# NF4 chunks dequantised in turned layout, and two chunks' accumulator in PSUM

## The chip, the core and the metric

The kernel runs on 1 core of a Trainium2 chip. The metric is device time in microseconds of one execution. Engines are named TensorE (PE), VectorE (DVE), ScalarE (ACT), GpSimd (POOL) and SyncE (SP, which issues most DMAs).

## What is computed

```python
x = x + xattn(layernorm(x), ctx, ctx, mask, Wq, Wk, Wv, Wo)   # 32 query heads, 8 key heads of 128, tanh cap 30
x = x + ffn(layernorm(x), w1, w2, w3)
# ffn: each weight is first quantised and dequantised in blocks of 64 along its rows
absmax = max(abs(flat), axis=1)              # flat = w.reshape(-1, 64)
idx = searchsorted(bounds, flat / absmax)    # 15 bounds, 16 NF4 codes
dq = NF4_CODE[idx] * absmax
out = (silu(x @ dq1.T) * (x @ dq2.T)) @ dq3.T
```

x is 8 x 128 x 512, w1 and w2 are 1376 x 512, w3 is 512 x 1376, all fp32. Blocks of 64 run along the 512 columns of w1 and w2 and along the 1376 columns of w3.

## The kernel before, in words

**Attention.** All 1024 tokens lie in SBUF as `xh` and `xl` (a high and a low fp32r part), features on partitions; a product of two fp32 matrices is three fp32r matmuls (high x high, high x low, low x high). After 16 key units and 16 value units the loop runs over 64 slots j = 8 kv + b (8 key heads, 8 batches). TensorE does in a slot: four transposes of the attention result into `trp`, `weighted_values(j+1)` (L610), `logits(j+3)` (L583), `q_unit(j+8)` (L506, 12 matmuls of 512 columns), `out_unit(j)` (L519, 12 matmuls; it waits for `at_lo`, written by VectorE's `atl`). VectorE does (L1151): `add_out(j-1)`, one NF4 add, `atl`, `sums`, more adds, the mask of j+3, `rope_parts(j+8)`, one more add. The query swap goes through a DMA of SP (L341) and the rope is added by GpSimd (L1290) two slots or more before its logits. Slots 56 to 63 have no `q_unit` and no NF4 work.

**NF4.** The weights are cut into 12 chunks of 128 x 1408 (22 blocks of 64). For a chunk c VectorE takes the blocks' maxima, replaces zeros and inverts (`nf_prepare`, L962); GpSimd multiplies the chunk by the inverse, a 128x22 tile read as a broadcast (`nf_normalise`, L1319, by `nf_blocks`, L1314); ScalarE makes 15 sign masks in u8, five buffers ahead (`nf_above_bound`, L755, the activation is L766); VectorE adds 15 steps to the accumulator (`nf_add`, L975; the first add is L984, the other 14 are L987: `scalar_tensor_tensor` with mask and accumulator in SBUF); GpSimd multiplies by the maxima (`nf_rescale`, L1324); SP stores the result to DRAM (`nf_store`, L327). `nf_before(slot)` (L259) spreads the places of the list, 16 to a chunk (15 adds and a gap), over slots 1 to 56 of the loop, the 22 hidden units and the first W3 pieces. Chunk 0 is the first of W3, 1 to 8 are W1 and W2, 9 to 11 the rest of W3.

**FFN.** 22 pieces of W1/W2 (`weights_in`, L435) and 11 of W3 (`w3_in`, L452) come back from DRAM into `stage`, rows of the weight on partitions. TensorE turns each with four transposes (`weight_transposes` L647, `w3_transposes` L705, both through `transpose4` L501, whose matmul is L503); ScalarE copies the high part out of PSUM (L881, L903), VectorE makes the low part (L1202, L1234). `hidden(n)` is 24 matmuls for gate and up of 512 tokens; the down projection is 11 rounds of 7 batches x 3 matmuls, and then batch 7 alone. W3 piece 8 needs the last chunk: its 13 last adds follow `hidden(21)` on VectorE.

PSUM has 8 banks: `prjs` 2, `bank` 3, `avp` 2, `trp` 1.

## Time and profile before

| | |
|---|---|
| median of 3 runs | 800.41 us (800.33 to 800.9) |
| profiled execution | 800.16 us, span 798.3 us |
| granted TensorE clock | 1.00 |
| ScalarE, GpSimd busy | 547.4 us, 367.3 us |
| DMA | 87.56 MB, mean 110 GB/s |
| stages by the trace | keys and values to about 150 us, loop with queries to 558, last head to 596, hidden units to 730, down projection to the end |

A share of busy time is of the whole span; TensorE's matmuls overlap, so its busy time says that it seldom stood still, not that it ran at its peak.

### The profile page before, as it was taken

The numbers are of one execution on the slowest core, as the hardware profiler recorded it, in microseconds if no ns is written. First come the engines' busy times: TensorE is split into PE (matmuls) and PEld (weight loads), VectorE is DVE, ScalarE is ACT, GpSimd is POOL, SyncE is SP. The second block draws the span as 40 slices with busy tenths as digits, with TensorE's granted clock in tenths as the row PEclk, the third lists the DMA queues.
The fourth block names the chain that finished last, engine by engine and source line by source line (L and its number), as shares of the span: only waits on it lengthen the run. The fifth ranks groups of instructions, "written<-read, shape, count | busy, mean of one in ns | idle before, by whom it ended". The sixth has DMA issues, their size and how long they took to land.

```text
span 798.3 us, 10879 instructions
## 1 busy us (share of the span) xinstructions
PE 789.0 (99%) x3810; PEld 635.9 (80%) x3810; DVE 661.7 (83%) x741; ACT 547.4 (69%) x859; POOL 367.3 (46%) x210
## 2 busy tenths in 40 slices
PE   8999999999999999999999999999999999999998
PEld 6777887878887788878888888888778888888876
DVE  6897755898999999898988889899574999999913
ACT  6467737787877868678787788786643877868510
POOL 4773265446637457366465365473100534435010
PEclk9999999999999999999999999999999999999999
DMA  9636456333432433425235335231401031412022
GB/s 335 199 129 201 131 155 169 110 99 93 139 107 77 154 97 112 129 71 171 79 84 152 92 93 165 80 103 47 136 14 40 27 126 54 124 28 76 14 69 106
DMA packets 60981, 87.56 MB, mean 110 GB/s; under 512 B 6272, under 2 KB 29952, under 8 KB 60928
## 3 DMA queue, kind: packets, MB, share of 16 engines
q1 hardware_dynamic: 59744, 84.06, 35.7%
q10 hardware_dynamic: 1184, 2.82, 1.0%
q8 instruction: 31, 0.51, 0.3%
q14 instruction: 22, 0.18, 0.1%
HBM read 51.00 MB, written 19.07 MB: 88 GB/s over the span
## 4 chain that ended last, share of the span: by engine, by line
PE 85%; DVE 6%; issue 5%; ACT 2%; DMA 1%; POOL 0%; POOLq 0%; SPq 0%; DVEq 0%
PE bank L530 7%; PE prjs L514 7%; PE prjs L516 7%; PE bank L532 7%; PE bank L531 7%; PE prjs L515 7%; PE bank L590 7%; PE avp L618 6%; PE trp L503 4%; PE bank L496 3%; PE bank L498 3%; PE bank L497 3%; PE prjs L498 2%; PE prjs L496 2%; PE prjs L497 2%
## 5 line engine op out<-in xcount | busy, mean ns | idle before, releaser
L1294 POOL TENSOR_TENSOR qT<-cs_loop,sw 128x512 f32<-128x512 f32 x56 | 107.2, 1915 | 183.4 <-DMA sw<-cs_loop 176.1
L514 PE MATMUL prjs<-xh,wqh 128*128 128x512 f32 x256 | 123.3, 482 | 0.0
L530 PE MATMUL bank<-woh,ath 128*128 128x512 f32 x256 | 100.8, 394 | 1.0 <-DVE atl L1161 0.9
L516 PE MATMUL prjs<-xh,wql 128*128 128x512 f32 x256 | 100.2, 391 | 0.0
L532 PE MATMUL bank<-woh,atl 128*128 128x512 f32 x256 | 99.9, 390 | 0.0
L531 PE MATMUL bank<-wol,ath 128*128 128x512 f32 x256 | 99.7, 389 | 0.0
L862 ACT ACTIVATE ath<-trp 128x512 fp32r<-128x512 f32 x64 | 38.2, 596 | 89.5 <-PE trp L503 89.5
L515 PE MATMUL prjs<-xl,wqh 128*128 128x512 f32 x256 | 99.5, 389 | 0.0
L995 DVE TENSOR_TENSOR cs_loop<-prjs,csq 128x1024 f32<-128x1024 f32 x56 | 68.3, 1220 | 21.4 <-PE prjs L516 21.2
L987 DVE SCALAR_TENSOR_TENSOR nfv<-nfq,nfv 128x1408 f32<-128x1408 uint8 x42 | 79.1, 1883 | 0.2
L850 ACT ACTIVATE nrm<-avp,rs 128x128 f32<-128x128 f32 x256 | 72.6, 372 | 7.0 <-DVE rs L1148 6.7
L987 DVE SCALAR_TENSOR_TENSOR nfx<-nfq,nfx 128x1408 f32<-128x1408 uint8 x42 | 75.9, 1807 | 0.0
L1388 POOL TENSOR_TENSOR hl<-hf,hh 128x512 fp32r<-128x512 f32 x22 | 33.8, 1538 | 75.7 <-ACT hh L901 75.7
L766 ACT ACTIVATE nfq<-nfv,bnd 128x1408 uint8<-128x1408 f32 x45 | 66.1, 1477 | 3.0 <-POOL nfv L1316 3.0
L618 PE MATMUL avp<-vcur,eb 128*128 128x129 f32 x512 | 67.7, 275 | 0.0
L1120 DVE TENSOR_TENSOR eb<-bank,maskf 128x512 f32<-128x512 f32 x64 | 43.1, 673 | 28.1 <-ACT bank L844 28.1
L590 PE MATMUL bank<-qT,kcur 128*128 128x512 f32 x128 | 65.6, 594 | 0.6 <-DVE eb L1120 0.6
L766 ACT ACTIVATE nfq<-nfa,bnd 128x1408 uint8<-128x1408 f32 x45 | 65.6, 1475 | 0.4 <-POOL nfa L1316 0.4
L515 PEld LDWEIGHTS prjs<-xl,wqh 128*128 128x128 f32 x256 | 48.2, 188 | 21.9 <-issue 13.6
L514 PEld LDWEIGHTS prjs<-xh,wqh 128*128 128x128 f32 x256 | 48.2, 188 | 21.4 <-issue 13.6
L618 PEld LDWEIGHTS avp<-vcur,eb 128*128 128x128 f32 x512 | 62.3, 192 | 0.5 <-issue 0.5
L1285 POOL TENSOR_TENSOR wol<-stage,woh 128x512 fp32r<-128x512 f32 x32 | 58.5, 1830 | 8.8 <-ACT woh L784 8.8
(187 smaller groups left out, 1966.6 us busy)
## 6 DMA issues: line engine op xcount, KB each, us to landing
sw<-cs_loop SPq DMA_DIRECT2D x112, 128.0 KB, 2.3
stage<-wq_pieces SPq DMA_DIRECT2D x32, 256.0 KB, 2.9
stage<-wo_pieces SPq DMA_DIRECT2D x32, 256.0 KB, 3.1
stage<-dq_scratch SPq DMA_DIRECT2D x32, 256.0 KB, 3.2
ks_scratch<-qT SPq DMA_DIRECT2D x16, 256.0 KB, 3.1
vs_scratch<-vst SPq DMA_DIRECT2D x16, 256.0 KB, 3.5
kcur<-ks_scratch SPq DMA_DIRECT2D x16, 256.0 KB, 2.9
vcur<-vs_scratch SPq DMA_DIRECT2D x16, 256.0 KB, 3.4
```

What stands on the lines that cost most here:

```text
L514: nc.tensor.matmul(o, wqh[:, g, k, :], xh[:, k, cs], start=k == 0, stop=False)
L515: nc.tensor.matmul(o, wqh[:, g, k, :], xl[:, k, cs], start=False, stop=False)
L516: last = nc.tensor.matmul(o, wql[:, g, k, :], xh[:, k, cs], start=False, stop=k == KT - 1)
L530: nc.tensor.matmul(o, ah, wh[:, g, :], start=g == 0, stop=False)
L531: nc.tensor.matmul(o, ah, wl[:, g, :], start=False, stop=False)
L532: last = nc.tensor.matmul(o, al, wh[:, g, :], start=False, stop=g == G - 1)
L590: nc.tensor.matmul(lgp[:, :], kcur[:, h, s * 128:(s + 1) * 128], qT[:, h, :, s * 128:(s + 1) * 128], start=True, stop=True).then_inc(logit ...
L618: av = nc.tensor.matmul(avp[:, g // 2, (g % 2) * (DH + 1):(g % 2 + 1) * (DH + 1)], eb[:, b % 2, g * 128:(g + 1) * 128], vcur[:, b, :], sta ...
L766: nc.scalar.activation(nf_mask(c, i), nf_bufs(c)[0][:, :], ACT.Sign, bias=bnd[:, i:i + 1])\
L850: last = nc.scalar.activation(nrm[:, j % 2, g * 128:(g + 1) * 128], avp[:, g // 2, (g % 2) * (DH + 1):(g % 2) * (DH + 1) + DH], ACT.Copy, ...
L987: op = nc.vector.scalar_tensor_tensor(acc[:, :], nf_mask(c, i), STEPS[i], acc[:, :], ALU.mult, ALU.add)
L1294: nc.gpsimd.tensor_tensor(dst, products(ru, slot)[:, 0, :], sw[:, slot, :], ALU.add).then_inc(roped, 1)
```

## The change

W1, W2 and W3 are given to the kernel a second time: `nf_chunks` now holds the chunks turned (what the matmuls want on partitions lies on partitions), `nf_natural` holds the old layout. VectorE takes maxima and inverses from the natural chunk (`nf_top`, 12 of them, all but two in the loop). For each chunk of W1/W2 TensorE turns the 128x44 tile of maxima and inverses (`turn_tops`), ScalarE copies it to `rows` (`tops_rows`), SP stores it to DRAM (`rows_store`), and broadcast loads bring it back as a full 128x1408 tile `scl` (`scale_load`), once with the inverses and once with the maxima. For W3 this is done for all four chunks at once, with 32 stores. GpSimd multiplies by `scl`. Adds, masks and stores of a chunk work on the turned layout; the pieces that come back need no transposes, and ScalarE and VectorE read them from `stage`. The order is now W1/W2 in chunks 0 to 7 and W3 in 8 to 11; the loop takes chunks 1 to 8 whole. PSUM `bank[2]`, `avp` and `trp` become one tensor `four`; 1408 columns of it are the accumulator of chunks 9 and 10 for the adds 0 to 13, and TensorE waits for the end of chunk 10 before its down matmuls of batch 4. `nomask` and `keep` share the memory of `eb`. The core of the diff:

```diff
-        bank = [ctx.enter_context(nc.psum_tensor(f"bank{i}", [128, 512], f32)) for i in range(3)]
-        avp = ctx.enter_context(nc.psum_tensor("avp", [128, 2, 512], f32))
-        trp = ctx.enter_context(nc.psum_tensor("trp", [128, 512], f32))
-        prj, prj2, lgp = [prjs[:, 0, :], prjs[:, 1, :]], [bank[0], bank[1]], bank[2]
+        bank = [ctx.enter_context(nc.psum_tensor(f"bank{i}", [128, 512], f32)) for i in range(2)]
+        four = ctx.enter_context(nc.psum_tensor("four", [128, 4, 512], f32))
+        lgp, avp, trp = four[:, 0, :], four[:, 1:3, :], four[:, 3, :]
+        prj, prj2 = [prjs[:, 0, :], prjs[:, 1, :]], [bank[0], bank[1]]
+        wide = four.rearrange("p b n -> p (b n)")[:, 0:CH]
         key_pair = [prjs, avp]
...
+        ADDS = [(c, i) for c in range(1, 12) for i in range(15)]
+        STREAM = [x for n, add in enumerate(ADDS)
+                  for x in ([(n // 9 + 2, None)] if n % 9 == 0 and n < 90 else []) + [add]]
+        LOOP_ITEMS = STREAM.index((9, 0))
...
-                return 122 * min(max(0, slot - 1), 55) // 55
+                return LOOP_ITEMS * min(max(0, slot - 1), 55) // 55
             if slot <= NSTEP + 2 * HT:
-                return 122 + 43 * min(max(slot - NSTEP - 2, 0), 20) // 20
-            return min(165 + max(0, 3 * (slot - NSTEP - 2 * HT) - 1), 16 * 11)
+                return LOOP_ITEMS + 34 * min(max(slot - NSTEP - 2, 0), 20) // 20
+            return min(LOOP_ITEMS + 34 + max(0, 3 * (slot - NSTEP - 2 * HT) - 1), len(STREAM))
...
+        def nf_norms(slot):
+
+            return [c + 1 for c, i in nf_items(slot) if i == 9 and c not in (8, 11)]
...
+            def rows_store(k):
+
+                sp.wait_ge(rows_done, k + 1)
+                if k < 8:
+                    sp.dma_start(tops_d[k], rows[0:44, 0, :]).then_inc(rows_out, 16)
                     return
-                at = 0
-                for lo, hi in W3_RUNS[max(0, c - NKV)]:
-                    sp.dma_start(dq3[:, 0:4 * HID].rearrange("p (a e) -> p a e", a=2)[:, :, lo * BLK:hi * BLK],
-                                 acc[:, :].rearrange("p (a e) -> p a e", a=2)[:, :, at * BLK:(at + hi - lo) * BLK])\
-                        .then_inc(nf_out, 16)
-                    at += hi - lo
+                for which in range(2):
+                    for part in range(4):
+                        to = tops3_d[which, part].rearrange("(n q a) r -> q a n r", q=2, a=2)
+                        for q, first in enumerate((part // 2, 21 + (part + 1) // 2)):
+                            for a in range(2):
+                                at = 44 * a + first
+                                sp.dma_start(to[q, a], rows[at:at + 21:2, which, :]).then_inc(rows_out, 16)
...
+            def scale_load(which, c):
+
+                if which == 0:
+                    if c in (8, 11):
+                        sp.wait_ge(nf_scaled, c)
+                    else:
+                        sp.wait_ge(nf_norm, c + 2 if c > 0 else 1)
+                else:
+                    wait(sp, nf_norm, c)
+                    wait(sp, nf_scaled, c if c in (1, 9) else c - 1)
+                if c < 8:
+                    sp.wait_ge(rows_out, 16 * (c + 1))
+                    for half in range(2):
+                        at = 22 * which + 11 * half
+                        sp.dma_start(scl[64 * half:64 * half + 64, :],
+                                     tops_d[c, at:at + 11, :].rearrange("r h -> (r h)").partition_broadcast(64))\
+                            .then_inc(scale_in, 16)
+                    return
+                sp.wait_ge(rows_out, 16 * 8 + 16 * 32)
+                for part in range(4):
+                    units = tops3_d[which, part, 11 * (c - 8):11 * (c - 7), :]
+                    sp.dma_start(scl[32 * part:32 * part + 32, :],
+                                 units.rearrange("u r -> (u r)").partition_broadcast(32)).then_inc(scale_in, 16)
...
+            def nf_transfers(slot):
+
+                for c in nf_norms(slot - 2):
+                    scale_load(0, c - 1)
+                for c in nf_finished(slot - 1):
+                    nf_store(c)
+                for c in nf_finished(slot - 2):
+                    if c < 7:
+                        nf_load(c + 2)
+                        scale_load(1, c + 2)
+                    if c == 7:
+                        scale_load(0, 8)
+                for k in nf_tops(slot - 2):
+                    if k < 8 or k == 11:
+                        rows_store(min(k, 8))
+                for k in nf_tops(slot - 1):
+                    if k < 11:
+                        nat_load(k + 1)
...
+                sp.wait_ge(nf_out, nf_stored(8 + ((n + 1) * D - 1) // CH))
+                wait(sp, wt_lo, m - 3)
+                sp.dma_start(stage[:, m % 4, :], dq3[:, n * D:(n + 1) * D]).then_inc(piece_in[m % 4], 16)
...
+            def turn_tops(k, j=0):
+
+                pe.wait_ge(nf_max, 3 * k + 3 if k < 8 else 36)
+                wait(pe, rows_done, k)
+                wait(pe, y_done, j)
+                out = tops_bank(k, j)
+                if k < 8:
+                    last = nc.tensor.transpose(out[0:44, 0:128], tops[:, :, :].rearrange("p w b -> p (w b)"), tab[:, 2, :])
+                else:
+                    for w in range(2):
+                        last = nc.tensor.transpose(out[0:88, w * 128:w * 128 + 128], tops3[:, w, :], tab[:, 2, :])
+                last.then_inc(nf_turned, 1)
...
+                for k in tops_turned(j - 1):
+                    pe.wait_ge(rows_done, k + 1)
...
-                    if last and b in (2, 3):
-                        weight_transposes(b - 2)
-                    if last and b == 5:
-                        weight_transposes(2)
+                    for k in tops_turned(j):
+                        turn_tops(k, j)
                     if last and b in (4, 6):
...
-            def weight_transposes(n):
-
-                pe.wait_ge(piece_in[n % 4], 16 * (STAGED + n // 4 + 1))
-                if n < 2:
-                    pe.wait_ge(cs_done, NK + NUNIT)
-                elif n == 2:
-                    pe.wait_ge(weights_done, NKV * B)
-                elif n == 3:
-                    pe.wait_ge(at_lo, NKV * B)
-                else:
-                    pe.wait_ge(wt_lo, n - 1)
-                transpose4(wt_bank(n), lambda k: stage[:, n % 4, k * 128:(k + 1) * 128]).then_inc(wt_done, 1)
-
             def token_transposes(b):
...
-            def w3_transposes(n):
-                m = 2 * HT + n
-                p = 128 if n < HT - 1 else HLAST
-                pe.wait_ge(piece_in[m % 4], 16 * (STAGED + m // 4 + 1))
-                wait(pe, wt_lo, m if n > 2 else m - 1)
-                transpose4(w3_bank(n), lambda i: stage[:, m % 4, i * 128:i * 128 + p], p).then_inc(wt_done, 1)
-
             for n in range(2, len(UNITS)):
-                t, half = UNITS[n]
-                if n > 3 and half == 0 and t < HT - 1:
-                    weight_transposes(2 * t + 2)
-                    weight_transposes(2 * t + 3)
-                if n == 2 * HT - 1:
-                    w3_transposes(0)
...
+                    if n == 0 and b == 4:
+                        pe.wait_ge(nf_acc, 15 * 11)
...
+            def tops_rows(k, j=0):
+
+                act.wait_ge(nf_turned, k + 1)
+                wait(act, rows_out, 16 * k)
+                src = tops_bank(k, j)
+                if k < 8:
+                    op = nc.scalar.activation(rows[0:44, 0, :], src[0:44, 0:128], ACT.Copy)
+                else:
+                    op = nc.scalar.activation(rows[0:88, :, :].rearrange("p w d -> p (w d)"), src[0:88, 0:256], ACT.Copy)
+                op.then_inc(rows_done, 1)
...
-                                     wt_bank(n)[:, :].rearrange("p (k h) -> p k h", k=KT), ACT.Copy).then_inc(wt_hi, 1)
+                                     stage[:, n % 4, :].rearrange("p (k h) -> p k h", k=KT), ACT.Copy).then_inc(wt_hi, 1)
...
+            def nf_top(k):
+
+                dve.wait_ge(nat_in, 16 * k + 16)
+                if k < 8:
+                    wait(dve, nf_turned, k)
+                    top, inverse = tops[:, 0, :], tops[:, 1, :]
+                    out = top.rearrange("p (half j) -> p j half", half=2)
+                    src = nat[:, :].rearrange("p (j half e) -> p j half e", half=2, e=BLK)
+                else:
+                    at = slice(22 * (k - 8), 22 * (k - 7))
+                    top, inverse = tops3[:, 0, at], tops3[:, 1, at]
+                    out, src = top, nat[:, :].rearrange("p (b e) -> p b e", e=BLK)
+                nc.vector.tensor_reduce(out, src, axis=AX.X, op=ALU.max, apply_absolute_value=True).then_inc(nf_max, 1)
+                dve.wait_ge(nf_max, 3 * k + 1)
                 nc.vector.scalar_tensor_tensor(nfg[:, :], top, 0.0, top, ALU.is_equal, ALU.add).then_inc(nf_max, 1)
-                dve.wait_ge(nf_max, 3 * c + 2)
-                nc.vector.reciprocal(nfr[:, :], nfg[:, :]).then_inc(nf_max, 1)
+                dve.wait_ge(nf_max, 3 * k + 2)
+                nc.vector.reciprocal(inverse, nfg[:, :]).then_inc(nf_max, 1)
...
+                n, to = 15 * c + i, nf_bufs(c)[1][:, :]
+                acc = wide if c in (9, 10) else to
+                if i < 14:
+                    to = acc
...
-                    op = nc.vector.scalar_tensor_tensor(acc[:, :], nf_mask(c, i), STEPS[i], acc[:, :],
+                    op = nc.vector.scalar_tensor_tensor(to, nf_mask(c, i), STEPS[i], acc,
...
+                if u == 8:
+                    nf_top(0)
...
-            def nf_blocks(buf, by):
-                blocks = buf[:, :].rearrange("p (b e) -> p b e", e=BLK)
-                return nc.gpsimd.tensor_tensor(blocks, blocks, by.rearrange("p (b o) -> p b o", o=1)
-                                               .to_broadcast([128, CH // BLK, BLK]), ALU.mult)
+            def nf_scale(buf):
+                return nc.gpsimd.tensor_tensor(buf[:, :], buf[:, :], scl[:, :], ALU.mult)
 
             def nf_normalise(c):
 
-                pool.wait_ge(nf_max, 3 * c + 3)
-                nf_blocks(nf_bufs(c)[0], nfr[:, :]).then_inc(nf_norm, 1)
+                pool.wait_ge(nf_in, 16 * c + 16)
+                pool.wait_ge(scale_in, scale_value(1, c))
+                nf_scale(nf_bufs(c)[0]).then_inc(nf_norm, 1)
 
             def nf_rescale(c):
 
                 pool.wait_ge(nf_acc, 15 * c + 15)
-                nf_blocks(nf_bufs(c)[1], nfm[:, c % 2, :]).then_inc(nf_scaled, 1)
+                pool.wait_ge(scale_in, scale_value(0, c))
+                nf_scale(nf_bufs(c)[1]).then_inc(nf_scaled, 1)
...
+                    if last and b == 3:
+                        nf_normalise(9)
...
-    parts = [np.pad(w, ((0, HT * 128 - HID), (0, 0))).reshape(HT, 128, D).transpose(1, 0, 2).reshape(128, NFW)
-             for w in (w1, w2)]
+    w12 = [np.pad(w, ((0, HT * 128 - HID), (0, 0))).reshape(HT, 128, KT, 128) for w in (w1, w2)]
+    by_unit = [w.transpose(3, 0, 2, 1).reshape(128, NFW) for w in w12]
+    by_hid = [w.transpose(1, 0, 2, 3).reshape(128, NFW) for w in w12]
+    third = np.pad(w3, ((0, 0), (0, HT * 128 - HID))).reshape(2, 128, 2, HT, 128).transpose(4, 3, 2, 0, 1)
     by_row = np.pad(w3.reshape(2, 128, 43, BLK).transpose(1, 0, 2, 3), ((0, 0), (0, 0), (0, 1), (0, 0)))
-    cols = [[b for lo, hi in runs for b in range(lo, hi)] for runs in W3_RUNS]
-    third = [by_row[:, :, (c + [43])[:11]].reshape(128, CH) for c in cols]
-    quarters = [w[:, q * CH:(q + 1) * CH] for q in range(4) for w in parts]
-    nf = np.concatenate([third[0]] + quarters + third[1:], axis=1)
+
+    def in_turn(ws, last):
+        return np.concatenate([w[:, q * CH:(q + 1) * CH] for q in range(4) for w in ws] + [last.reshape(128, NFW)], axis=1)
+
+    nf, nat = in_turn(by_unit, third), in_turn(by_hid, by_row)
...
```

## Rows read from the trace of the kernel before

**Rows 1.** Busy time, share and instructions of each engine, from the page.

```profile
PE 789.0 (99%) x3810; PEld 635.9 (80%) x3810; DVE 661.7 (83%) x741; ACT 547.4 (69%) x859; POOL 367.3 (46%) x210
```

**Rows 2.** TensorE's waits: for whom, us in total, times, longest.

```profile
PE bank L530 <- DVE atl L1161: 0.9, 4, 0.3
PE trp L503 <- DMA stage<-dq_scratch: 0.7, 1, 0.7
...
PE trp L503 <- DVE nrm L1073: 0.3, 1, 0.3
```

**Rows 3.** Busy time by stage: PE, PEld, DVE, ACT, POOL, clock, DMA share, GB/s.

```profile
150.00:558.00 408.00, 407.51 (x2020) 327.52 (x2019) 371.98 (x398) 319.10 (x531) 223.55 (x118) 1.00 0.38 106
...
618.00:730.00 112.00, 112.00 (x531) 93.35 (x530) 106.59 (x84) 83.98 (x97) 50.65 (x26) 1.00 0.21 66
```

**Rows 4.** Line L503 alone: duration ns min/median/max, first and last start.

```profile
L503 PE MATMUL trp<-tab,stage x80: 270/272/327, 598.5 to 777.8; 128*128 128x128 f32 x76, 128*96 128x128 f32 x4
...
L503 PE MATMUL bank<-tab,stage x44: 270/272/273, 586.2 to 729.5; 128*128 128x128 f32 x44
...
L503 PE MATMUL prjs<-tab,stage x8: 272/273/273, 570.1 to 575.8; 128*128 128x128 f32 x8
```

**Rows 5.** Chain of work, hidden units: start us, us, what.

```profile
706.17 0.44 PE bank L503 x4
...
709.81 0.23 PE bank L496
```

**Rows 6.** Timeline of VectorE, one slot of the loop: start us, us.

```profile
327.74 0.69 DVE L1142 TENSOR_TENSOR y<-bank,y 128x512 f32<-128x512 f32 x1
328.35 1.62 DVE L987 SCALAR_TENSOR_TENSOR nfx<-nfq,nfx 128x1408 f32<-128x1408 uint8 x1
329.88 0.69 DVE L1161 TENSOR_TENSOR atl<-trp,ath 128x512 fp32r<-128x512 f32 x1
...
331.26 0.69 DVE L1120 TENSOR_TENSOR eb<-bank,maskf 128x512 f32<-128x512 f32 x1 [0.61 <-ACT bank L844]
332.67 1.23 DVE L995 TENSOR_TENSOR cs_loop<-prjs,csq 128x1024 f32<-128x1024 f32 x1 [0.72 <-PE prjs L516]
...
335.40 0.69 DVE L1142 TENSOR_TENSOR y<-bank,y 128x512 f32<-128x512 f32 x1
```

**Rows 7.** Timeline of VectorE: an nf_prepare and what follows it.

```profile
620.65 1.61 DVE L968 TENSOR_REDUCE nfm<-nfw 128x22 f32<-128x1408 f32 x1
...
622.72 1.56 DVE L987 SCALAR_TENSOR_TENSOR nfv<-nfq,nfv 128x1408 f32<-128x1408 uint8 x1
```

**Rows 8.** Timeline: a multiply of GpSimd and the add beside it.

```profile
626.11 3.94 POOL L1316 TENSOR_TENSOR nfw<-nfw,nfr 128x1408 f32<-128x1408 f32 x1
...
627.74 3.79 DVE L987 SCALAR_TENSOR_TENSOR nfv<-nfq,nfv 128x1408 f32<-128x1408 uint8 x1
```

**Rows 9.** Groups of GpSimd: busy us, mean ns, idle before.

```profile
L1294 POOL TENSOR_TENSOR qT<-cs_start,sw 128x512 f32<-128x512 f32 x8 | 10.3, 1291 | 29.7 <-DMA sw<-cs_start 29.6
...
L1316 POOL TENSOR_TENSOR nfx<-nfx,nfm 128x1408 f32<-128x1408 f32 x3 | 7.7, 2551 | 0.0
```

**Rows 10.** SP: its longest wait, and one issue of a small DMA.

```profile
SPq L346 <- DVE cs_loop L995: 298.7, 56, 7.3
...
3.54 0.43 SPq L367 DMA_DIRECT2D mt<-mask_t  x1
```

**Rows 11.** DMA issues by line: count, KB each, median us to landing.

```profile
dq_scratch<-nfx SPq DMA_DIRECT2D x3, 704.0 KB, 4.1
```

**Rows 12.** Chain of work at the end: VectorE, GpSimd, store and load.

```profile
731.77 0.69 DVE hf L1231
...
758.09 2.60 POOLq L48
...
761.11 2.82 DMA dq_scratch<-nfv
763.95 2.94 DMA stage<-dq_scratch
```

186 lines of the change are left out of this document (99 added, 87 removed).

## The prediction

> **What bounds the kernel now.** I read the page first: TensorE is busy 789.0 of 798.3 us, VectorE 83%, ScalarE 69%, GpSimd 46% [rows 1]. A TensorE share that high only says that it seldom stood still, so next I read its waits: the loop loses 0.9 us to `atl` from VectorE, the end of the kernel 0.7 us to the DMA of a W3 piece, the start 0.3 us to a normalised token [rows 2]. So every instruction taken out of TensorE's stream shortens the kernel by its own time, as long as nobody else becomes late. Who is near to being late is what the table by stages shows: in the attention loop VectorE works 371.98 of 408 us (91%), in the hidden units 106.59 of 112 (95%), TensorE is full in both [rows 3]. ScalarE has 78% at most and GpSimd 55% in the same rows. The reader should carry two facts on: TensorE sets the pace by a small margin, and VectorE stands right behind it.
>
> **What is taken from TensorE.** Before, each of the 22 W1/W2 pieces and 11 W3 pieces that comes back from DRAM is turned by four fp32 transposes: 80 + 44 + 8 = 132 transposes [rows 4], 33 groups of four. A group holds TensorE for 0.44 us in the chain of work [rows 5]: 33 x 0.44 = 14.5 us, all of it in a full stream and so all on the path. With them goes the 0.7 us in which transposes waited for the piece [rows 2]. Removed: **15.2 us**. ScalarE and VectorE now read the piece from `stage` in SBUF instead of from PSUM; 128x512 operations take the same 0.6 to 0.7 us in either form, nothing follows.
>
> **What TensorE gets.** Nine `turn_tops`, one transpose each and two for the last; a transpose in a row costs a fourth of 0.44 = 0.11 us [rows 5], and a lone one has its start and its wait in full: I take 0.2 us, between 0.1 and 0.5. 9 x 0.2 = **+1.8 us** (0.9 to 4.5). What they wait for (`nf_max`, and `y_done` of the unit before) is finished by VectorE one slot earlier or before the `atl` that TensorE waits for anyway: zero.
>
> **VectorE in the loop, where the gain can be given back.** The order of the adds changes. Before, 122 places of the list in 55 slots hold 115 adds and 7 `nf_prepare`; after, 130 places hold 120 adds and 10 `nf_top`. A loop slot lasts 7.66 us: `y` at 327.74 and again at 335.40. In it an add takes 1.55 us (328.35 to the `atl` at 329.9), and a slot with two adds leaves VectorE 0.61 + 0.72 = 1.33 us idle, so its work is 6.3 us [rows 6]. A maximum with its inverse takes 622.72 - 620.65 = 2.07 us [rows 7]. New load: 5 x 1.6 + 3 x 2.07 = 14.2 us. A slot with three adds then holds 7.9 us and one with two adds and a top 8.4 us, both over 7.66; three-item slots rise from 12 of 55 to 20 of 55.
> VectorE and GpSimd also block each other. The scale multiply took 3.94 us beside an add, and the add that began at 627.74 took 3.79 us: it ended 1.5 us after GpSimd's operation ended at 630.05 [rows 8], while alone they take 2.55 [rows 9] and 1.55 us. That is a lock held for a whole instruction. (The Trainium skill, page SBUF — State Buffer, section Who interferes with whom, states this rule: a VectorE instruction with two SBUF inputs contends with a GpSimd one that reads SBUF, and one with at most one SBUF input does not. By that rule, the trace agrees: 3.79 us.) The change makes GpSimd's multiply read a full 128x1408 second operand, `scl`, where before it was a broadcast 128x22. No row has this form. The lower end is 2.55 us; the upper end is the two-operand 128x512 add at 1.29 us, scaled by columns: 3.55 us [rows 9]. I take 3.2, nearer to the form that has both operands full. (The Trainium skill, page GPSIMD Engine Reference, reconciling with measured numbers, gives 4497 ns for 2048 fp32 columns of tensor_tensor; an estimate by columns is 3.1 us, and the sum would move by under 1 us.) Sixteen of them lie in the loop: 16 x 0.65 = 10 us more lock.
> How much reaches TensorE? `out_unit(j)` needs `atl(j)`, which a lightly loaded VectorE finishes some 2.5 us early, because `q_unit` runs between. A heavy slot (8.4) with a lock of 3.2 us before its add is 4 us over its 7.66, and TensorE loses the part over 2.5, about 1.5 us; half of that where the slot holds three adds (7.9) or starts with less delay. I take 8 of the 16 multiplies as meeting such a slot, at 0.7 us each: **+5.5 us**. The ends: 0, if VectorE's 36 us of idle time take it all; 14.2 + 10 - 5 = 19 us, if every added microsecond beyond a part that meets PSUM operations arrives.
>
> **The queues.** SP issues per chunk one `nat_load`, one `rows_store` and four broadcast loads more, 6 x 0.43 = 2.6 us in 7 slots, while SP waited 298.7 us in 56 swaps, 5.3 us each [rows 10]: hidden. The last `rows_store` is 32 DMAs in one slot, 32 x 0.43 = 14 us; behind it are queued the swap of the next query unit and a weight piece. The swap is made two slots (15 us) before its unit's logits need it, and the backlog drains by 5 us a slot: 0 to 5 us, I take 0 to 1 inside the 5.5 above. A 704 KB store lands in 4.1 us [rows 11]; the broadcast loads have the same size, are issued one slot before the rescale that needs them, and what waits behind a late one on GpSimd is the rope, with the same two slots of room: zero. The DMA share is 0.38 in the loop [rows 3]; 36 more transfers of 0.72 MB add a tenth or so.
>
> **Hidden units.** Chunks 9 and 10 accumulate in PSUM from step 0 to 13. A PSUM operand takes these adds out of the lock; they stay near 1.6 us by the 128x512 PSUM rows (0.69 us for `hf`) [rows 12]: 1408 / 512 x 0.6 = 1.65. With the three tops gone and 34 adds where there were 40 or so, VectorE's 106.59 us [rows 3] lose 3 x 2.07 + 6 x 1.6 = 16 us, more than TensorE's stage shortens. TensorE did not wait for VectorE here before, so this brings nothing by itself; it is cover.
>
> **The last chunk.** After `hidden(21)` at 731.77 VectorE has 13 adds and low parts until 758; GpSimd rescales until 760.69; store and load take 2.82 + 2.94 us [rows 12]. After the change the same 13 adds follow, but TensorE, without its transposes, wants W3 piece 8 already 8 x 21 x 0.228 = 38.3 us after its first down matmul, where it was 8 x (4.79 + 0.44) = 41.8 (a matmul in the stream takes 0.23 us [rows 5]). The chain is 0.7 to 2.5 (silu, multiply) + 25.5 + 3.2 + 0.4 + 4.1 (the store is now one transfer of 704 KB) + 2.9 + 1.5 (high and low part) = 38.3 to 40.1 us. So this new wait costs 0 to 2 us: **+1.0**.
> **The start.** `nf_top(0)` (2.07 us) comes into the key units before the first normalised token, for which TensorE waits already (0.3 us) [rows 2]; between 0 and the whole 2.07, most of it into slack between the key units: **+0.6**.
>
> **Sum.** -15.2 + 1.8 + 5.5 + 1.0 + 0.6 = -6.3 us. The profiled execution took 800.16 us (span 798.3 and 1.86 around it), the median of the runs 800.41, so the profile stands for them: 800.2 - 6.3 = **793.9 us**.
>
> **Rivals.**
> (a) The cover holds: VectorE's idle time and the 2.5 us of room absorb everything in the loop. For it speaks that before only 0.9 us came through at 91%. -15.2 + 1.8 + 0 to 2.5: 785.5 to 789.5, middle 787.5. Chance 0.27.
> (b) VectorE becomes the bound of the loop. Place: `atl` in front of `out_unit`. Price: the 19 us above, 807 us; middle 803. It decides from a multiply of 3.55 us on, or when give-back passes 13.4 us, the size of the net gain elsewhere. For it: 95 to 96% load after the change; against: VectorE also loses its own waits when late. Chance 0.2, three quarters of it above 802.
> (c) The SP burst of 32 stores and the waits of the broadcast loads delay ropes by more than two slots; TensorE waits at `logits` once or a few times. 3 to 8 us on top of the forecast: 797 to 802. Chance 0.08.
> (d) The PSUM accumulator does not free VectorE as said, adds are longer than 2 us: the hidden units have 1.5 us a unit to spare, so it only delays the last chunk, +1 to 3 us, inside the forecast's range.
> The forecast, 790 to 798 us: 0.45.
>
> **Range and chances.** From 785.5 (the whole of a) to 801.5 (with c and the lower part of b) about 0.83. A measurement tells about 0.2% (1.6 us) from no change, so "same" is 798.8 to 802.0: 0.08 from (b), (c) and the forecast's edge. Faster 0.75, slower 0.17.
>
> **What would show it.** Right: no group `trp<-tab,stage`; TensorE busy about 774 us; its wait list led by `atl` with 5 to 9 us; multiply rows (L1316's successor) with a least duration of 3.1 to 3.3 us; adds in `four` at 1.6 us whatever GpSimd does; VectorE at 94 to 97% in the loop. Wrong: `atl` waits under 2 us (then a) or over 12 us (b); a wait of `lgp` on the rope near the 41st slot (c); the down projection waiting over 3 us for `stage`.

## The result and the profile after

The changed kernel takes **827.6 us** (median of 4 runs, 827.3 to 830.1) where the kernel before takes 800.5 us: ratio 1.034, interval [1.032, 1.037]. The forecast was 793.9 us, in a range from 785.5 to 801.5. The result lies 33.7 us above the forecast and 26 us above the range, and the sign was wrong: faster was forecast. The page of the changed kernel begins:

```profile
span 825.4 us, 10794 instructions
...
PE 785.5 (95%) x3688; PEld 627.6 (76%) x3688; DVE 664.4 (80%) x741; ACT 550.1 (67%) x868; POOL 379.5 (46%) x210
...
PEclk9999999999999999999999979999989999997999
```

TensorE does 122 matmuls less than in [rows 1] (3688 for 3810), yet its span is 27.1 us longer and its share has fallen from 99 to 95%. Three slices of the clock row fall below 9: TensorE stood still at three places. What it waited for (us in total, times, longest), to be held against [rows 2]:

```profile
PE bank L624 <- DVE atl L1262: 10.3, 9, 4.8
PE prjs L805 <- DVE w3l L1343: 9.6, 1, 9.6
PE four L595 <- ACT nrm L942: 6.5, 2, 6.1
PE four L646 <- DVE tops L1068: 2.9, 2, 2.3
```

Three single waits of 4.8, 9.6 and 6.1 us are most of it. A table by stage, from the first starts of the lines of the output unit, of the hidden units and of the down projection, shows where they lie. It is made from one profiled execution of each kernel, and the last two columns are experiments that follow. The wait of 9.6 us counts to the hidden units, since it ends where the down projection starts.

| us | before | after | e4_three | e12_all |
|---|---|---|---|---|
| start, to the first output unit | 132.8 | 136.4 | 136.9 | 136.0 |
| attention loop, to hidden(0) | 462.9 | 487.5 | 471.0 | 465.7 |
| hidden units | 133.8 | 134.2 | 124.4 | 124.3 |
| down projection and end | 68.8 | 67.3 | 68.0 | 68.8 |
| span | 798.3 | 825.4 | 800.3 | 794.8 |

**Stall 1: the burst of small stores, slot 41.** SP's own timeline (start us, us, what; a time on SP is the time of issuing, not of the transfer):

```profile
458.69 0.60 SPq L427 DMA_DIRECT2D sw<-cs_loop  x1
459.33 0.58 SPq L514 DMA_DIRECT2D kcur<-ks_scratch  x1
459.96 25.16 SPq L376 DMA_DIRECT2D tops_scratch<-rows  x32
485.17 0.49 SPq L332 DMA_DIRECT2D stage<-wo_pieces  x1
485.77 0.53 SPq L426 DMA_DIRECT2D sw<-cs_loop  x1
```

32 stores of `rows_store(8)` hold SP for 25.16 us, 0.79 us each. Behind them in its queue are a piece of Wo and a swap. Who was idle until these came (in brackets the idle time and what ended it), from the timelines of ScalarE, GpSimd, VectorE and TensorE:

```profile
488.26 0.63 ACT L861 ACTIVATE woh<-stage 128x512 fp32r<-128x512 f32 x1 [8.18 <-DMA stage<-wo_pieces]
489.51 1.27 POOL L1393 TENSOR_TENSOR qT<-cs_loop,sw 128x512 f32<-128x512 f32 x1 [18.46 <-DMA sw<-cs_loop]
490.88 1.23 DVE L1094 TENSOR_TENSOR cs_loop<-prjs,csq 128x1024 f32<-128x1024 f32 x1 [9.62 <-POOL qT L1393]
489.97 1.12 PE L595 MATMUL four<-tab,nrm 128*128 128x128 f32 x4 [6.12 <-ACT nrm L942]
```

ScalarE works in order: `high()` of the late piece stands ahead of the four `nrm` that TensorE needs next. So the first victim on TensorE's path was not the rope but the weight piece. The stall costs more than its wait, as the windows show (PE, PEld, DVE, ACT, POOL busy; then the granted clock):

```profile
484.00:486.00 2.00, 0.00 (x0) 0.00 (x0) 0.00 (x0) 0.00 (x0) 0.00 (x0) 1.00 0.04 9
486.00:488.00 2.00, 0.00 (x0) 0.00 (x0) 0.00 (x0) 0.00 (x0) 0.00 (x0) 0.72 0.80 218
488.00:496.00 8.00, 5.51 (x16) 4.06 (x17) 5.12 (x4) 5.41 (x9) 3.87 (x4) 0.50 0.97 243
496.00:498.00 2.00, 2.00 (x8) 1.59 (x7) 2.00 (x4) 1.52 (x5) 2.00 (x1) 0.72 0.47 99
498.00:500.00 2.00, 2.00 (x11) 1.65 (x10) 1.12 (x2) 2.00 (x4) 2.00 (x2) 1.00 0.00 0
```

TensorE idles from 483.9 to 490.0. Its clock goes to 0.50 (1.2 GHz) while it idles, stays there until after 496 although TensorE works again from 490 on, and is at 1.00 from 498. From one output unit to the next it takes 17.86 us instead of 7.66: 10.2 us lost, for a wait of 6.1.

**Stall 2: the last head.** SP's store of chunk 8 waits until GpSimd has rescaled it, and the first four FFN pieces are queued behind that store and the load of four scales. GpSimd's row, then SP's:

```profile
583.55 3.20 POOL L1414 TENSOR_TENSOR nfv<-nfv,scl 128x1408 f32<-128x1408 f32 x1
```

```profile
586.78 0.34 SPq L357 DMA_DIRECT2D dq_scratch<-nfv  x1
587.23 0.38 SPq L351 DMA_DIRECT2D nfw<-nf_chunks  x1
587.72 2.30 SPq L399 DMA_DIRECT2D scl<-tops_scratch  x4
590.11 0.84 SPq L534 DMA_DIRECT2D stage<-dq_scratch  x2
```

The piece comes late: ScalarE waits 2.9 us for it, its low part on VectorE starts at 598.08, and meets the multiply that began at 597.03: 2.64 us instead of 0.7. `atl` stands behind it:

```profile
601.97 0.79 PE L624 MATMUL bank<-woh,ath 128*128 128x512 f32 x1 [4.84 <-DVE atl L1262]
```

**Stall 3: the start of the down projection.** The same with chunk 10: SP waits for the multiply that ends at 748.7, then issues a store, four scales, and only then W3 piece 0:

```profile
748.75 0.34 SPq L357 DMA_DIRECT2D dq_scratch<-nfy  x1
749.18 2.28 SPq L399 DMA_DIRECT2D scl<-tops_scratch  x4
751.56 6.84 SPq L548 DMA_DIRECT2D stage<-dq_scratch  x5
```

```profile
758.07 0.80 PE L805 MATMUL prjs<-w3h,hh 128*128 128x512 f32 x1 [9.60 <-DVE w3l L1343]
```

### The profile page after: what moved, and what is told of

It is laid out like the page before. It is cut to its first block, busy times and chain, and to the rows that moved or that the text cites. A ratio compares the mean times of both kernels' runs of the same rounds, so it can differ in the third digit from the quotient of the medians.

```text
span 825.4 us, 10794 instructions
## 1 busy us (share of the span) xinstructions
PE 785.5 (95%) x3688; PEld 627.6 (76%) x3688; DVE 664.4 (80%) x741; ACT 550.1 (67%) x868; POOL 379.5 (46%) x210
## 4 chain that ended last, share of the span: by engine, by line
PE 69%; DVE 12%; issue 5%; DMA 4%; SPq 4%; POOL 2%; ACT 2%; DVEq 0%; POOLq 0%; ACTq 0%
PE prjs L606 5%; PE prjs L608 5%; PE prjs L607 5%; PE bank L624 5%; PE bank L626 5%; PE bank L625 5%; PE four L699 5%; PE four L729 4%; PE bank L588 3%; PE bank L590 3%; PE bank L589 3%; SPq L376 3%; DVE nfv L1086 3%; DVE nfx L1086 3%; PE four L595 3%
## 5 line engine op out<-in xcount | busy, mean ns | idle before, releaser
L1393 POOL TENSOR_TENSOR qT<-cs_loop,sw 128x512 f32<-128x512 f32 x56 | 102.4, 1829 | 176.1 <-DMA sw<-cs_loop 162.1
L942 ACT ACTIVATE nrm<-four,rs 128x128 f32<-128x128 f32 x256 | 72.7, 371 | 20.0 <-DVE rs L1249 19.7
L954 ACT ACTIVATE ath<-four 128x512 fp32r<-128x512 f32 x64 | 38.2, 596 | 71.0 <-PE four L595 71.0
L1086 DVE SCALAR_TENSOR_TENSOR nfv<-nfq,nfv 128x1408 f32<-128x1408 uint8 x42 | 83.8, 1996 | 0.0
L1086 DVE SCALAR_TENSOR_TENSOR nfx<-nfq,nfx 128x1408 f32<-128x1408 uint8 x42 | 82.5, 1965 | 0.0
L624 PEld LDWEIGHTS bank<-woh,ath 128*128 128x128 f32 x256 | 48.6, 190 | 28.2 <-DVE atl L1262 15.9
L729 PE MATMUL four<-vcur,eb 128*128 128x129 f32 x512 | 68.6, 278 | 0.0
L699 PE MATMUL four<-qT,kcur 128*128 128x512 f32 x128 | 66.6, 603 | 1.2 <-DVE eb L1221 0.7
L1384 POOL TENSOR_TENSOR wol<-stage,woh 128x512 fp32r<-128x512 f32 x32 | 63.1, 1974 | 4.9 <-ACT woh L861 4.8
L729 PEld LDWEIGHTS four<-vcur,eb 128*128 128x128 f32 x512 | 63.2, 194 | 0.5 <-issue 0.5
```

Source lines behind the costliest of these rows:

```text
L624: nc.tensor.matmul(o, ah, wh[:, g, :], start=g == 0, stop=False)
L699: nc.tensor.matmul(lgp[:, :], kcur[:, h, s * 128:(s + 1) * 128], qT[:, h, :, s * 128:(s + 1) * 128], start=True, stop=True).then_inc(logit ...
L729: av = nc.tensor.matmul(avp[:, g // 2, (g % 2) * (DH + 1):(g % 2 + 1) * (DH + 1)], eb[:, b % 2, g * 128:(g + 1) * 128], vcur[:, b, :], sta ...
L942: last = nc.scalar.activation(nrm[:, j % 2, g * 128:(g + 1) * 128], avp[:, g // 2, (g % 2) * (DH + 1):(g % 2) * (DH + 1) + DH], ACT.Copy, ...
L1086: op = nc.vector.scalar_tensor_tensor(to, nf_mask(c, i), STEPS[i], acc, ALU.mult, ALU.add)
L1393: nc.gpsimd.tensor_tensor(dst, products(ru, slot)[:, 0, :], sw[:, slot, :], ALU.add).then_inc(roped, 1)
```

## The experiments

The theory: SP's queue, not VectorE, took the time, at three places that have nothing to do with each other. Rival: VectorE is the bound, and the stalls would come back elsewhere. Four of the kernels multiply by other scales than the reference (e1_one_store and e4_three for W3, e6_broadcast and e13_before_full for more); the rest of their work is as described. A gain is a difference of medians where nothing else is said.

**One place at a time, then all three.** e1_one_store replaces the 32 stores by two (same bytes, in an order that is not the one W3's scales need):

```diff
-                for which in range(2):
-                    for part in range(4):
...
+                for half in range(2):
+                    sp.dma_start(tops3_d[half].rearrange("p u r -> (p u r)").rearrange("(k x) -> k x", k=88),
+                                 rows[0:88, :, :].rearrange("p w d -> p (w d)")).then_inc(rows_out, 16)
```

> The changed kernel with the 32 stores of the W3 maxima made as 2 stores of 88 rows of 1 KB each; the values land in the wrong order, so the scales of the W3 chunks are not the reference's, while every transfer, wait and instruction behind them stays. Theory (SP's queue): the 32 stores hold SP for 25.2 us, the swap and the weight piece behind them come late, TensorE stands 6.1 us and then runs at 1.2 GHz, 10.2 us in all between two out units; without them 816 to 819 us. Rival (VectorE and the lock make the loop slow, the late pieces hide inside that): 824 us or more.

Measured 821.1 us, ratio 1.025 [1.022, 1.028]: 6.5 us less, under what was expected. The wait for `nrm` is 0.2 us. By stage the loop is 8.5 us shorter (479.0 for 487.5), but the start is 2.5 us longer (138.9 for 136.4), with the same code; the part on e4_three says why.

e2_w3_early issues `w3_in(0)` to `w3_in(3)` at hidden unit 19, ahead of the transfers of chunk 10:

```diff
+                if n == 19:
+                    for k in range(4):
+                        w3_in(k)
                 for c in nf_norms(NSTEP + n - 1):
...
-            for n in range(8):
+            for n in range(4, 8):
                 w3_in(n)
```

> The changed kernel with the first four W3 pieces issued at hidden unit 19, ahead of the store of chunk 10 and its wait for GpSimd. Theory (SP's queue): the 9.6 us in which TensorE waits for the first low part go, and the slow clock after them (some 3 us): 813 to 816 us. Rival (the down projection is bound by the last chunk's adds anyway, which end at 787.8 us): the wait moves to piece 8, 822 us or more.

Measured 820.8 us, 1.026 [1.023, 1.028]: 6.8 us less, half of what was expected. The wait for `w3l` falls from 9.6 to 1.1 us, and the hidden units from 134.2 to 124.4 us, 9.8 us less; the start is again longer, 138.7 us.

e3_head_early issues `weights_in(0)` to `weights_in(3)` at the first batch of the last head, ahead of the store of chunk 8, and no longer at the second batch:

```diff
+                    if last and b == 0:
+                        sp.wait_ge(nf_out, nf_stored(7))
+                        for n in range(4):
+                            weights_in(n)
                     nf_transfers(j)
```

> The changed kernel with the first four W1/W2 pieces issued one slot earlier, ahead of the store of chunk 8, the load of chunk 9 and its four scale loads. Theory (SP's queue): ScalarE no longer waits 2.9 us for the piece in front of the tanh, the 4.84 us stop and the slow clock go: 7 to 8 us less, 819 to 821 us. Rival (VectorE's low part, 2.64 us long beside GpSimd's multiply, is what makes atl late): 825 us or more.

Measured 822.5 us, 1.028 [1.026, 1.031]: 5.1 us less, again under the expectation; the longest wait for `atl` is 1.0 us, where it was 4.8. The loop is 6.3 us shorter (481.2) and the start takes 138.8 us.

e4_three is the three together.

> The changed kernel with the three edits of the other runs together (the W3 scales are again not the reference's). Theory: the three costs add, -10.2 -13 -7.6 = -31 us: 795 to 799 us, below the kernel before, and what is left of atl waits in the loop is 4 to 6 us. Rival (one bound stands behind another): more than 804 us.

Measured 804.1 us, 1.005 [1.003, 1.006]. That misses the expected 795 to 799 us and lies at the rival's edge of 804. The three gave 6.5, 6.8 and 5.1 us alone (18.4) and 23.4 together: the order on SP cost 23.4 of the 27.2 us. The forecast without the three stalls would still have been 10 us too low.

The three don't hide one another, though 18.4 and 23.4 look like it. By stage they gave 8.5, 9.8 and 6.3 us, 24.6 in sum, and the spans of the changed kernel and e4_three lie 25.1 us apart (825.4 and 800.3). The difference is in the start. TensorE stands still there for 2.3 us at the first turned maximum, in every one of these kernels. What follows varies from kernel to kernel, as the windows of e4_three and of e5_spread (below) show, in the columns of stall 1, with the granted clock third from the end:

```profile
38.00:42.00 4.00, 4.00 (x19) 3.30 (x18) 2.09 (x6) 1.57 (x4) 1.29 (x1) 1.00 0.25 94
```

```profile
38.00:42.00 4.00, 4.00 (x12) 3.15 (x12) 2.30 (x5) 0.00 (x0) 1.28 (x1) 0.58 0.35 131
```

In the profiled executions of the changed kernel, e4_three and e6_broadcast the clock stays at 1.00, and the first output unit starts at 136.4 to 137.7 us. In those of e1_one_store, e2_w3_early, e3_head_early, e5_spread, e7_sbuf_acc, e9_halves and e10_shift it is at 0.50 for 2 to 3 us or so around the end of the wait and behind it, and the output unit starts at 137.8 to 139.3. So two times can differ by up to 3 us, with and without that fall, before the edit has done anything. The four runs of e4_three show it too: the one at a mean clock of 1.000 took 802.4 us, the other three 804.1 to 804.4.

**The burst in the kernel before.** e8_before_burst puts the same 32 stores (from `tab`, to an array that nobody reads) behind slot 41 of the kernel before, nothing else.

> The kernel before, with only the 32 small stores (21 rows or so of 512 bytes each, from the table in SBUF to a scratch array that nobody reads) put on SP behind the transfers of slot 41. Theory (the burst by itself holds SP for 25 us and the swap behind it makes TensorE stand still, whose clock then falls): 8 to 12 us slower than before, 808 to 812 us, with granted clock 0.50 in the slot after. Rival (the burst costs only as much as it does because the changed kernel has more transfers queued around it): at most 804 us.

Measured **818.0 us**, 1.022 [1.021, 1.024]: 17.6 us slower, nearly double what was expected. The rival fell, but so did the size. The timelines give the chain, the same burst, then GpSimd, ScalarE, VectorE and TensorE:

```profile
450.20 25.54 SPq L437 DMA_DIRECT2D burst_scratch<-tab  x32
```

```profile
479.65 1.26 POOL L1305 TENSOR_TENSOR qT<-cs_loop,sw 128x512 f32<-128x512 f32 x1 [24.36 <-DMA sw<-cs_loop]
480.87 2.54 POOL L1327 TENSOR_TENSOR nfv<-nfv,nfr 128x1408 f32<-128x1408 f32 x1
483.45 1.47 ACT L777 ACTIVATE nfq<-nfv,bnd 128x1408 uint8<-128x1408 f32 x1 [20.59 <-POOL nfv L1327]
485.44 0.69 DVE L1172 TENSOR_TENSOR atl<-trp,ath 128x512 fp32r<-128x512 f32 x1 [17.99 <-ACT ath L873]
486.18 0.79 PE L541 MATMUL bank<-woh,ath 128*128 128x512 f32 x1 [16.06 <-DVE atl L1172]
```

Here a scale multiply happened to stand behind the late rope on GpSimd. ScalarE waited for its result with `ath` queued behind. The rope had its two slots of room; the multiply behind the rope had none. What a blocked queue costs depends on what else is due in those 25 us: 10 us in the one kernel, 17.6 in the other.

**The whole change with a clean queue.** e5_spread keeps the places that W3's scales need: 16 stores, the rows of the maxima and of the inverses in one, four stores in each of four slots, and the two earlier issues. The broadcast load of chunk 8's inverses moves behind them.

```diff
-                        rows_store(min(k, 8))
...
+                for part in range(4):
+                    if 11 in nf_tops(slot - 2 - part):
+                        rows3_store(part)
...
```

> The changed kernel, whole, with the three places on SP mended: the stores of the last rows are 16 instead of 32 (both weights' rows in one), put four by four into four slots; the first four W3 pieces are asked for at hidden unit 19; the first four W1/W2 pieces of the last head are asked for ahead of the store of chunk 8. Theory (the three stalls come from SP's order alone): as with one store, 803 to 806 us; no wait of TensorE over 2.5 us. Rival (any row of small stores in the loop makes the swap late, however spread): a wait for nrm or for a rope of 2 us or more near the slots 42 to 45, 808 us or more.

Measured 804.1 us, 1.005 [1.004, 1.006]: as with one store. SP's row for the first part has 3.92 us for four stores, the other three parts 3.4 us, so each store takes 0.84 to 0.98 us, and four in a slot of 7.66 us do no harm:

```profile
463.53 3.92 SPq L377 DMA_DIRECT2D tops_scratch<-rows  x4
```

**The accumulator in PSUM.** e7_sbuf_acc is e5_spread with `acc = to` for all chunks.

> As the spread kernel, but chunks 9 and 10 accumulate in SBUF as the others do. Theory (VectorE has room in the hidden units, so the PSUM accumulator is only cover): within 1.5 us of the spread kernel; the adds of these two chunks go from 1.62 us to some 1.6 to 2.0 us in the mean. Rival (PSUM keeps the last chunk on time): chunk 11 is late, the down projection waits for it, 3 us or more slower than the spread kernel.

Measured 805.9 us, 1.006 [1.005, 1.008], against 804.1: 1.8 us, just over the theory's 1.5 and under the rival's 3, and the intervals overlap. So PSUM brings a small gain at most. But the adds show a lock between VectorE and GpSimd: while one of them works, the other can be held up for a whole instruction, as the add of 3.79 us beside a multiply in [rows 8]. Groups of VectorE, hidden units, first e5_spread, then e7_sbuf_acc:

```profile
L1099 DVE SCALAR_TENSOR_TENSOR four<-nfz,four 128x1408 f32<-128x1408 uint8 x26 | 42.2, 1622 | 1.0
```

```profile
L1099 DVE SCALAR_TENSOR_TENSOR nfy<-nfz,nfy 128x1408 f32<-128x1408 uint8 x14 | 33.3, 2378 | 0.6
L1099 DVE SCALAR_TENSOR_TENSOR nfa<-nfz,nfa 128x1408 f32<-128x1408 uint8 x14 | 29.9, 2137 | 0.6
```

In PSUM each add takes 1.61 to 1.63 us. In SBUF the adds take 1.6 us at the least and 2.1 to 2.4 in the mean, more than the 1.6 to 2.0 expected; 2.73 us, for one, when an add begins together with a product of 1.29 us on GpSimd. The unit has the room for either.

**What the multiply costs.** e6_broadcast is e4_three with the multiply's second operand read as 22 columns by broadcast.

> The kernel with the three places taken away (804.1 us), with GpSimd's multiply reading 22 columns of scl by broadcast, as the kernel before did, instead of the full 1408; the scales are not the reference's in it, the transfers are unchanged. Theory (a third of the loop's give-back is the longer multiply, which holds VectorE): multiply rows fall from 3.2 to some 2.55 us, the waits for atl from 5.3 to about 2 to 3 us, 801 to 802.5 us. Rival (the give-back is VectorE's three more items of work alone): 803.5 us or more, waits for atl still over 4.5 us.

Measured **796.0 us**, 0.995 [0.993, 0.996]: 8.1 us less, where 2 to 3 were expected. The multiply fell as expected (GpSimd's group of `nfv`, e4_three then e6_broadcast: busy, mean ns):

```profile
L1414 POOL TENSOR_TENSOR nfv<-nfv,scl 128x1408 f32<-128x1408 f32 x9 | 29.6, 3290 | 22.2 <-DVE nfv L1086 22.2
```

```profile
L1415 POOL TENSOR_TENSOR nfv<-nfv,scl 128x1408 f32<-128x1408 f32 x9 | 23.5, 2615 | 22.2 <-DVE nfv L1086 22.2
```

The wait of the matmuls for `atl` fell from 5.3 to 2.5 us, as expected, and that is far from 8.1 us. Part of the rest is in a row that I had not read: the weight loads (PEld) wait for the same `atl`, and stand idle two to three times as long. Three views of waits, of before, e4_three and e6_broadcast:

```profile
PEld bank L530 <- DVE atl L1161: 3.1, 6, 0.7
```

```profile
PEld bank L624 <- DVE atl L1262: 11.3, 14, 1.4
```

```profile
PEld bank L624 <- DVE atl L1262: 6.1, 8, 1.4
```

The loop takes 462.9, 471.0 and 465.3 us in the three. Between the last two, 5.2 us of the weight loads' wait go with 5.7 us of the loop. The spans lie 6.4 us apart; the medians' 8.1 us holds 1.7 us more, since three of the four runs of e4_three took 1.7 to 2.0 us longer than its profiled one.

e13_before_full is the mirror: the kernel before, with a full 1408-column operand in the multiplies of the first seven heads.

> The kernel before, where in the attention loop's first seven heads GpSimd's scale multiply reads a full 128x1408 operand (a piece of xh) instead of 22 columns by broadcast; the scales are not the reference's in it, all else is unchanged. Theory (the longer multiply by itself holds VectorE long enough to be late with atl): multiply rows of 3.2 us and more, the weight loads' wait for atl from 3.1 to 9 us or more, 804 to 808 us. Rival (it costs only together with the three more maxima and five more adds of the changed kernel): 800.5 to 802.5 us.

Measured 802.7 us, 1.003 [1.002, 1.005]: 2.7 us, which is under the theory's range and just over the rival's. The weight loads' wait for `atl` doubles, 3.1 to 6.5 us. The loop is 3.2 us longer (466.1), for 14 long multiplies; in the changed kernel the same form cost the loop 5.7 us, for 16. So over half of it needs nothing but the longer multiply. That the rest comes with the changed order of the work is an inference; no run separates it.

**Load or hold?** Four changes to e5_spread. e9_halves cuts each multiply in two of 704 columns:

```diff
-                return nc.gpsimd.tensor_tensor(buf[:, :], buf[:, :], scl[:, :], ALU.mult)
+                for at in (0, CH // 2):
+                    last = nc.gpsimd.tensor_tensor(buf[:, at:at + CH // 2], buf[:, at:at + CH // 2],
+                                                   scl[:, at:at + CH // 2], ALU.mult)
+                return last
```

> As the spread kernel (804.1 us), with each scale multiply on GpSimd cut into two of 704 columns. Theory (what reaches TensorE is the longest single time for which one multiply holds VectorE, 3.2 us against 1.6): 799 to 802 us, waits for atl from 6.0 to 3 us or less. Rival (the total time under the lock counts, which the cut leaves as it is): 803 to 805.5 us, waits for atl still 5 us or more.

Measured 800.9 us, 1.000 [0.999, 1.001]: 3.3 us gained, as expected. GpSimd's multiply time does not fall but rises, from 82.9 to 96.7 us over all chunks (`nfv` alone from 31.0 to 32.9); only the single hold gets shorter. The matmuls' wait for `atl` goes from 6.0 to 3.6 us, where 3 or less was expected, and that of the weight loads from 12.2 to 8.1 us (e5_spread, then e9_halves):

```profile
PEld bank L637 <- DVE atl L1275: 12.2, 15, 1.4
```

```profile
PEld bank L637 <- DVE atl L1275: 8.1, 12, 1.6
```

e10_shift moves the last 8 adds of chunk 8 into the hidden units (`LOOP_ITEMS = STREAM.index((8, 7))`, scales (1, 9) before (0, 8), and the transfers that belong to them).

> As the spread kernel (804.1 us), with the last 8 adds of chunk 8 moved out of the attention loop into the hidden units (130 places in 55 slots become 122, 34 adds in the hidden units become 42). Theory (VectorE's load in the loop is the bound): 8 adds of 1.9 us less there, waits for atl down to 2 to 3 us, 800 to 802 us, and nothing lost in the hidden units, where VectorE is busy 71%. Rival (the load isn't what matters, only the multiply that falls ahead of atl): 803 us or more.

Measured 803.6 us, 1.003 [1.002, 1.005]: 0.6 us, within the scatter, as the rival said. The loop takes 471.2 us, where e5_spread has 471.5. With 8 adds less there (VectorE 395.8 of 440 us instead of 410.3), the weight loads wait for `atl` as before:

```profile
PEld bank L634 <- DVE atl L1272: 12.4, 16, 1.7
```

So the theory that load alone bounds the loop falls. While the multiply is whole, its length counts and these 8 adds don't.

e11_start turns the first maxima one key unit later (`if u == 10: turn_tops(0)`).

> As the spread kernel (804.1 us), with the first turned maximum one key unit later on TensorE. Theory (TensorE stood still for 2.3 us at it because nf_top(0) on VectorE wasn't done, and lost the same again in its clock or in what came after): that wait goes, 801 to 802.5 us. Rival (the same VectorE work is late for the next key unit anyway): 803.5 us or more, with a wait of the same size at the next unit.

Measured 801.7 us, 1.001 [1.000, 1.002]: 2.4 us gained, as expected. The 2.3 us wait for `tops` is gone, and the clock stays at 1.00 there; the start takes 135.0 us, where the profiled e5_spread, with the fall of the clock, has 139.3. TensorE had stood behind VectorE's 2.3 us of maximum and inverse (35.17 to 37.44 us in the changed kernel), in its own order.

e12_all is all of these together.

> The whole change with its three places on SP mended, the multiply in halves, the 8 adds moved and the first turn later. Theory (the causes are separate): the single gains add up, 795 to 798 us, faster than the kernel before (800.4). Rival (they are the same microseconds, VectorE is full in the loop all the same): 800 us or more.

Measured **796.6 us**, 0.995 [0.993, 0.996], as expected and 0.5% faster than the kernel before. The loop takes 465.7 us, where e9_halves has 468.6. The loop of e12_all differs from that of e9_halves by the 8 adds and what belongs to them, so with the multiply in halves they seem to be worth 2.9 us, though they were worth 0.3 us of loop with the multiply whole. The loop is 471.5 and 472.9 us in two kernels that have it alike (e5_spread, e7_sbuf_acc), so 2.9 us is twice the scatter seen; no run makes these two changes alone. The busy row of e12_all:

```profile
PE 777.5 (98%) x3688; PEld 621.7 (78%) x3688; DVE 651.0 (82%) x741; ACT 550.9 (69%) x868; POOL 376.2 (47%) x234
```

e15_quarters cuts the multiply in four of 352 columns instead.

> As the kernel with all mended (796.6 us), with each multiply in four of 352 columns instead of two of 704. Theory (the longest single hold counts): a further 1 to 2 us, 794.5 to 796 us. Rival (the hold is short enough already, each piece only adds its own start): 796.5 to 799 us.

Measured 796.7 us, 0.995 [0.994, 0.997]: no further gain, as the rival said. At 1.7 us the hold is short enough here.

e14_rope_first puts the multiplies behind the low part and the rope of their slot on GpSimd.

> As the kernel with all mended (796.6 us), with GpSimd's scale multiplies put behind the weight's low part and the rope of their slot instead of ahead of them. Theory (what is late is the add ahead of atl, so a multiply that begins later in the slot meets adds that nobody waits for at once): 793 to 796 us, the weight loads' wait for atl from 5.9 to under 4 us. Rival (a later multiply makes ScalarE's signs and so the next adds late): 797.5 us or more, with waits of ScalarE's nfq for the multiply.

Measured 821.9 us, 1.027 [1.024, 1.029]: 25 us slower, for the rival's reason but far beyond its size. The theory failed on its own sign, too: the weight loads' wait for `atl` rose from 5.9 to 7.2 us. So which add meets which multiply is not shown to be what counts. GpSimd waits for the swap, ScalarE for the multiply, and TensorE for `nrm`, which is queued behind on ScalarE; one of its four stalls, 16.8 us in all:

```profile
318.18 1.30 POOL L1403 TENSOR_TENSOR qT<-cs_loop,sw 128x512 f32<-128x512 f32 x1 [5.00 <-DMA sw<-cs_loop]
319.43 3.37 POOL L1425 TENSOR_TENSOR nfv<-nfv,scl 128x704 f32<-128x704 f32 x2
```

```profile
322.83 1.47 ACT L853 ACTIVATE nfq<-nfv,bnd 128x1408 uint8<-128x1408 f32 x1 [6.37 <-POOL nfv L1425]
```

```profile
327.02 1.11 PE L605 MATMUL four<-tab,nrm 128*128 128x128 f32 x4 [3.96 <-ACT nrm L952]
```

## Why the prediction was wrong

**The removed transposes: right.** From hidden(0) to the end e4_three takes 192.4 us where before took 202.6: 10.2 us less. 29 of the 33 groups lie there [rows 4], at 0.44 us [rows 5] 12.8 us, and the new waits take the difference (the weight loads' rows have 4.1 us there, where before had 1.1). It is the changed kernel that hid it: 134.2 + 67.3 us, with stall 3 inside.

**The turns: right in size, wrong on their wait.** A turn takes 0.27 to 0.29 us in its row, I took 0.2. That what it waits for is done in time failed for the first: 2.3 us, and 2.4 us by e11_start. The start lost 3.6 us, and 5 to 6.5 us in the executions where the clock fell at that wait; the forecast had 0.6 because it laid `nf_top(0)` into slack and not in front of a TensorE instruction.

**The queues: the step that failed.** The term was put at nothing, "hidden", for three reasons, each wrong in its own way.
- The price of an issue. "32 x 0.43 = 14 us" took [rows 10]'s 0.43 us of one plain load; these stores take 0.79 us each, 25.2 us in all.
- Who is behind. I followed the swap to the rope and its two slots of room, and made that rival (c), at 0.08. The weight piece in the same queue, and ScalarE that stands in order at `high()` with `nrm` behind, were named ("and a weight piece") and not priced. Nor was that a stall goes on costing while the clock is down. (c) was the right mechanism with the wrong place and size: the sign that I gave, `lgp` waiting for the rope, measures 0.5 us; the stall showed at `nrm`, 10.2 us.
- What SP waits for. I counted the new DMAs' issue time alone. But `nf_store(8)` and the store of chunk 10 wait for a rescale of GpSimd, and in the changed order the loads of the first FFN and W3 pieces stand behind them. Together with stall 1 this is 23.4 us by e4_three, seven tenths of the error. No step of the prediction walked SP's program around the chunk's end, and none of the rivals has these two stalls. A sign of being wrong that I set does name one of them, the down projection waiting over 3 us for `stage`: it waited 9.6 us, by way of `w3l`.

The DMA engines' load was put too low as well: their share in the loop rose from 0.38 to 0.57, not by "a tenth or so". No harm of it is seen: e12_all has 0.56 there and is faster than the kernel before.

**VectorE in the loop: about the right size, wrongly argued.** Against the forecast's +5.5 us stands what e4_three shows: the loop is 8.1 us longer, 9.9 without the four groups (1.8 us) that went from it. The turns take some 2 us of it, so 7 to 8 us are left for VectorE. The multiply's second operand makes 5.7 us of them (e6_broadcast), which leaves some 2 us for the three maxima and five adds. The multiply came as forecast, 3.2 us at the least. The upper end, 19 us, and the reason (load, 94 to 97%) were off: e10_shift took load away without effect, e6_broadcast and e9_halves shortened the hold and gained 8.1 and 3.3 us. (Load isn't nothing either: with the multiply in halves, moving the same adds goes with 2.9 us less of loop, as e12_all shows.) The signs that I set, waits for `atl` of 5 to 9 us in the loop, were met (5.3 in e4_three), and understated the loss by half, since the weight loads' row (11.3) is the one that follows the time more closely. The row was there before the change too, with 3.1 us where I read 0.9 [rows 2].

**The hidden units: right.** Adds in PSUM take 1.61 to 1.63 us whatever GpSimd does, as forecast, and VectorE's room there is cover only: taking the accumulator out of PSUM moves at most 1.8 us. (The Trainium skill, page SBUF — State Buffer, section Who interferes with whom, says that an instruction of VectorE with at most one SBUF input does not contend with GpSimd, outside the 2-port perf modes, which `tensor_scalar` can enter. The adds agree: 1.62 us with one such input, 2.1 to 2.4 with two.) The limit matters: the first add of a chunk is a `tensor_scalar` with one SBUF input, takes 0.88 us at its shortest, and took 3.92 us when it began beside a multiply of GpSimd (e5_spread, the first add of chunk 11):

```profile
732.88 3.92 DVE L1096 TENSOR_SCALAR nfv<-nfz 128x1408 f32<-128x1408 uint8 x1
```

The two first adds that write to `four` take 1.62 us.

**The last chunk: right for its own wait, with others left out.** +1.0 us, 0 to 2, was for a wait of piece 8. In e4_three TensorE's weight loads wait 2.3 us for `w3l` and 1.8 us for `hf` after hidden(21), 4.1 us. Of this the last wait for `w3l`, 0.94 us at 773.8, is the one where piece 8 is due; the waits for `hf` and for two earlier pieces the forecast did not have. So the down projection and what follows shrink by 0.8 us only, though their transposes went.

**Sum.** 793.9 + 23.4 (stalls) + 3.0 (start) + 3.1 (last chunk and `hf`: 4.1 for 1.0) + about 2 (VectorE) = 825.4, against 827.6 measured. The 23.4 us come from medians and the other terms from profiles. With 25.1 us, the difference of the two profiles, the sum is 827.1 us. One sum of the prediction doesn't come out of its own terms: rival (a), -15.2 + 1.8 + 0 to 2.5, gives 786.8 to 789.3 us, not 785.5 to 789.5; nothing hangs on it.

What stays open: e12_all is 1.3 us faster than the sum of its parts (797.9). That fits the 2.9 us which its loop is shorter than that of e9_halves, but is about as large as these runs scatter. Why the same longer multiply costs the changed kernel's loop more than the one before (5.7 and 3.2 us) isn't settled: e10_shift has as many places in the loop as the kernel before, and its waits stayed. Nor is why the same wait of 2.3 us in the start is followed by a lower clock in some executions and not in others.
